# Two mixtures of experts: choice and counts made per sequence in the stage of the gate logits, normalised tiles and the inversion's products written by ScalarE, list of experts made over partitions

## What is computed

```
x = x + recurrent_block(norm(x))        # projections, gated linear recurrence, feed-forward
x = x + moe0(norm(x))                   # 16 experts of width 256, 2 per token, relu
x = x + attention(norm(x))              # 16 heads of 8, rotary
x = x + block(norm(x))                  # attention, x1 = norm(.)*g1+be1, moe1(x1), norm
# moe0: logits = y @ Wg + bg + bias; the two highest; weights = softmax of these two
# moe1: p = softmax(x1 @ Wg + bg) over 8 experts of width 512 (gelu); the two highest,
#       divided by their sum
# out[token] = sum over its two experts of weight * (act(y @ W1[e] + b1[e]) @ W2[e] + b2[e])
```

## Time and profile before

| | us |
|---|---|
| median of 3 runs (2523.53 to 2530.19) | 2529.16 |
| the profiled execution | 2531.16 |
| its span | 2529.3 |
| TensorE busy | 2030.4 (80%) |
| VectorE busy | 1988.9 (79%) |
| ScalarE busy | 1507.4 (60%) |
| GpSimd busy | 593.3 (23%) |

### The profile page before, as it was taken

How to read it: one execution, slowest core, us unless ns; L and a number is a source line. 1 busy time by engine, 2 the same in 40 slices (tenths; PEclk the granted TensorE clock), 3 DMA queues, 4 the chain that set the end, 5 groups by cost and what they waited for, 6 DMA issues and landing times. The chain is left out here.

```text
span 2529.3 us, 45491 instructions
## 1 busy us (share of the span) xinstructions
PE 2030.4 (80%) x16896; PEld 958.9 (38%) x16896; DVE 1988.9 (79%) x3319; ACT 1507.4 (60%) x2948; POOL 593.3 (23%) x702
## 2 busy tenths in 40 slices
PE   6999675882479999999999579999999999369910
PEld 4888464771222222222222322222222222359910
DVE  7887647565679999999994779999999994576635
ACT  5553330340118988989888218988989889105500
POOL 2444300667520000000000340000000000316555
PEclk9999885895769999999999769999999999559955
DMA  5000010243341010110100351010110100302211
GB/s 192 1 1 1 0 32 11 78 91 78 115 147 32 20 42 19 33 42 20 42 6 10 110 153 31 21 42 19 32 42 20 42 6 10 122 10 74 64 51 55
DMA packets 94411, 121.16 MB, mean 48 GB/s; under 512 B 23664, under 2 KB 56560, under 8 KB 93936
## 3 DMA queue, kind: packets, MB, share of 16 engines
q1 hardware_dynamic: 73712, 78.92, 11.3%
q0 software_dynamic: 8960, 18.37, 3.0%
q10 hardware_dynamic: 11520, 20.98, 2.7%
HBM read 69.70 MB, written 42.99 MB: 45 GB/s over the span
## 5 line engine op out<-in xcount | busy, mean ns | idle before, releaser
L1489 DVE TENSOR_REDUCE mx<-psum 128x1 f32<-128x1024 f32 x1024 | 1175.1, 1216 | 82.2 <-PE psum L1377 81.3
L1466 ACT ACTIVATE p<-psum 128x512 f32<-128x512 f32 x2048 | 1102.5, 596 | 108.8 <-PE psum L1399 66.2
L1411 PE MATMUL psum<-p,v_ext 128*32 128x256 f32 x8192 | 656.5, 392 | 39.3 <-ACT p L1466 39.2
L1377 PE MATMUL psum<-ks,qs 64*128 64x512 bf16 x2048 | 636.0, 395 | 53.1 <-DVE mx L1489 29.9
L1399 PE MATMUL psum<-qs,ks 64*128 64x512 bf16 x2048 | 630.6, 383 | 1.5 <-ACT p L1466 1.3
L1411 PEld LDWEIGHTS psum<-p,v_ext 128*32 128x32 f32 x8192 | 162.2, 108 | 474.2 <-ACT p L1466 254.6
L1279 POOL CAST m_near<-mx 128x16 bf16<-128x16 f32 x128 | 25.1, 196 | 1080.9 <-DVE mx L1489 1076.8
L1399 PEld LDWEIGHTS psum<-qs,ks 64*128 64x128 bf16 x2048 | 123.4, 93 | 404.0 <-ACT p L1466 368.0
L746 ACT ACTIVATE hid<-psum,stage 128x128 f32<-128x128 f32 x448 | 132.1, 366 | 180.3 <-PE psum L716 180.3
L690 POOL DMA_INDIRECT x_in<-n_rows,token_of x152 | 166.2, 1093 | 296.3 <-POOLq L85 229.2
L1377 PEld LDWEIGHTS psum<-ks,qs 64*128 64x128 bf16 x2048 | 118.7, 94 | 115.3 <-DVE mx L1489 81.3
(11 more groups left out here) (229 smaller groups left out, 2120.7 us busy)
## 6 DMA issues: line engine op xcount, KB each, us to landing
qs<-qk_parts SPq DMA_DIRECT2D x128, 104.0 KB
ks<-qk_parts SPq DMA_DIRECT2D x128, 104.0 KB
qk_parts<-piece__1 ACTq DMA_DIRECT2D x40, 256.0 KB, 3.7
qk_parts<-piece__2 ACTq DMA_DIRECT2D x40, 256.0 KB, 3.5
answers<-y_out SPq DMA_DIRECT2D x152, 64.0 KB, 1.5
ew<-in_moe SPq DMA_DIRECT2D x1, 5136.0 KB, 18.8
ew<-in_moe SPq DMA_DIRECT2D x1, 4624.0 KB, 13.9
n_rows<-n_all SPq DMA_DIRECT2D x8, 512.0 KB, 3.2
```

Source lines behind the costliest of these rows:

```text
L1377: pe.matmul(psum[:, bank, :], a["qs"][r, g % NKF, j % KM, i * P:(i + 1) * P], a["ks"][r, g % NKF, j % KM, k * HALF:(k + 1) * HALF], start= ...
L1411: last = pe.matmul(psum[GR * j:GR * j + VW, O_BANK, q], t["v_ext"][:, b * NT + i, VE * (h0 + j):VE * (h0 + j) + VW], a["p"][:, (GH * s + j ...
L1466: act.activation(a["p"][:, n % NP, :], psum[:, S_BANK + n % NS, :], ACT.Exp, scale=DH ** -0.5)\
L1489: dve.tensor_reduce(a["mx"][:, g % 2, h, j, 0, c:c + 1], psum[:, bank:bank + 2, :].rearrange("p a c -> p (a c)"), AX.X, ALU.max)\
```

## The change

- `gate_logits` becomes `choose`. The normalised tiles are written by ScalarE (`normalise`), with scale 1/std and a shift that VectorE computes by one more small operation in `scale`. ScalarE's order is root(b+1), normalise(b), both copies of b; in the second mixture the four exponentials stand behind all of it.
- The choice, the one-hot rows and their sum (`pick`) are made per sequence by VectorE in that stage: in the first mixture behind each sequence's logits, in the second for all four behind the last logits. TensorE counts per sequence (`count`), behind all its other work, into banks 6 and 7.
- `route` begins with the counts. The weights of the mix are made at its end. The list of experts is made with the tile's number along the partitions (128x16 or 128x8), and TensorE turns it at the beginning of `invert`, where VectorE reads it behind its last chunk.
- In `invert` VectorE writes 8 comparisons in one instruction (`hi_eq`, 128 x 8 x 80 or 72), and ScalarE multiplies each with the token's number.
- `ew` of both mixtures is loaded behind `consts` at the start of the mixture. `consts` has its own semaphore, which VectorE and TensorE wait for within `choose`; `ew` is waited for ahead of `route`.

```diff
 def route(nc, t, layer, E, tiles):
...
+    with stage(nc, "step", "to_exp", "exped") as (block, step, to_exp, exped):
+        if not layer:
+            @block.scalar
+            def _(act):
+                act.wait_ge(to_exp, 1)
+                act.activation(tmp[:, :, 1], tmp[:, :, 0], ACT.Exp).then_inc(exped, 1)
...
+            if not layer:
+                dve.tensor_tensor(tmp[:, :, 0], mx[:, :, 1], mx[:, :, 0], ALU.subtract).then_inc(to_exp, 1)
+            link(dve.tensor_copy(cnt[:, :, :], psum[:, 7, 0:TE].rearrange("p (t e) -> p e t", e=E)))
...
             dve.tensor_copy(t["slot_of"][:, :, :], sel[:, :, :])
+            link(dve.tensor_scalar(t["ended"][:, 0:E], end[:, 0:E], t["token"][:, 0:1], None, ALU.is_lt))
+            link(dve.tensor_reduce(t["who"][:, :], t["ended"][:, 0:E], AX.X, ALU.add))
+            if layer:
+                link(dve.tensor_tensor(tmp[:, :, 0], mx[:, :, 0], mx[:, :, 1], ALU.add))
+                link(dve.reciprocal(tmp[:, :, 1], tmp[:, :, 0]))
+                link(dve.tensor_tensor(wt[:, :, :], mx[:, :, 0:2], tmp[:, :, 1:2].to_broadcast([P, T, 2]), ALU.mult))
+            else:
+                dve.wait_ge(exped, 1)
+                link(dve.tensor_scalar(tmp[:, :, 0], tmp[:, :, 1], 1.0, None, ALU.add))
+                link(dve.reciprocal(wt[:, :, 0], tmp[:, :, 0]))
+                link(dve.tensor_tensor(wt[:, :, 1], tmp[:, :, 1], wt[:, :, 0], ALU.mult))
...
+    hi_eq = t["hi_eq"]
+    with stage(nc, "step", "lo_ready", "eq_ready", "hi_ready", "used", "named") as \
+            (block, step, lo_ready, eq_ready, hi_ready, used, named):
+        @block.scalar
+        def _(act):
+            for n in range(pairs):
+                if n % G == 0:
+                    act.wait_ge(eq_ready, n // G + 1)
+                if n >= 2 * G:
+                    act.wait_ge(used, n - 2 * G + 1)
+                act.activation(t["hi_hot"][:, n % (2 * G), 0:tiles], hi_eq[:, n // G % 2, n % G, :], ACT.Copy,
+                               scale=t["token"][:, n // 2:n // 2 + 1]).then_inc(hi_ready, 1)
...
-                for n in range(c * G, (c + 1) * G):
-                    dve.tensor_scalar(t["hi_hot"][:, n % (2 * G), 0:tiles], t["iota"][:, 0:tiles],
-                                      flat(hi)[:, n:n + 1], t["token"][:, n // 2:n // 2 + 1],
-                                      ALU.is_equal, ALU.mult).then_inc(hi_ready, 1)
+                if c >= 2:
+                    dve.wait_ge(hi_ready, G * (c - 1))
+                dve.tensor_tensor(hi_eq[:, c % 2, :, :], t["iota"][:, 0:tiles].unsqueeze(1).to_broadcast([P, G, tiles]),
+                                  flat(hi)[:, c * G:(c + 1) * G].unsqueeze(2).to_broadcast([P, G, tiles]),
+                                  ALU.is_equal).then_inc(eq_ready, 1)
+            dve.wait_ge(named, 1)
+            dve.tensor_scalar(t["expert_of"][:, 0:tiles], psum[0:1, 3, 0:tiles], float(t["E"] - 1), None, ALU.min)
             dve.wait_ge(used, pairs)
             link(dve.tensor_scalar(t["token_f"][:, 0:tiles], psum[:, 2, 0:tiles], -1.0, 0.0, ALU.add, ALU.max))
             dve.tensor_copy(t["token_of"][:, 0:tiles], t["token_f"][:, 0:tiles])
...
+            pe.transpose(psum[0:1, 3, 0:P], t["who"][:, :], t["ident"][:, :]).then_inc(named, 1)
             for n in range(pairs):
                 if n % G == 0:
                     pe.wait_ge(lo_ready, n // G + 1)
...
+def choose(nc, t, w, layer, E, x, n):
...
+            def normalise(b):
+                act.wait_ge(scales_ready, b + 1)
+                for i in range(NT):
+                    act.activation(n[b][:, i, :], src[b][:, i, :], ACT.Identity, scale=t["rstd"][:, b % 2, i:i + 1],
+                                   bias=t["shift"][:, b % 2, i:i + 1]).then_inc(tile_ready, 1)
+            def copy_turned(b):
                 for h in range(NH):
                     act.wait_ge(turned, NT * b + TPH * (h + 1))
                     if b:
                         act.wait_ge(done, NH * (b - 1) + h + 1)
                     act.activation(t["y_t"][:, h * HALF:(h + 1) * HALF], psum[:, 2 * (b % 2) + h, :], ACT.Copy)\
                         .then_inc(y_copied, 1)
+            def exponent(b):
+                act.wait_ge(to_exp, b + 1)
+                v = lg[:, b * NT:(b + 1) * NT, :]
+                act.activation(v, v, ACT.Exp).then_inc(exped, 1)
+            root(0)
+            for b in range(B):
+                if b + 1 < B:
+                    root(b + 1)
+                normalise(b)
+                copy_turned(b)
+                if layer and b == B - 1:
+                    for c in range(B):
+                        exponent(c)
...
+            def count(b):
+                pe.wait_ge(both_ready, b + 1)
+                c, v = slice(b * NT * E, (b + 1) * NT * E), both[:, b * NT:(b + 1) * NT, :].rearrange("p t e -> p (t e)")
+                pe.matmul(psum[:, 6, c], t["before"][:, :], v, start=True, stop=True)
+                pe.matmul(psum[:, 7, c], t["ones"][:, :], v, start=True, stop=True)
             for b in range(B + 1):
                 if b < B:
                     turn(b)
                 if b:
                     logits(b - 1)
+            pe.wait_ge(t["consts_loaded"], 16 * (layer + 1))
+            for b in range(B):
+                count(b)
...
+            def scale(b):
                 r, m, v = rstd[:, b % 2, :], tmp[:, 0, :], t["var"][:, b % 2, :]
                 dve.wait_ge(std_ready, b + 1)
+                if b >= 2:
+                    dve.wait_ge(tile_ready, NT * (b - 1))
                 link(dve.reciprocal(r, t["std"][:, b % 2, :]))
...
                 link(dve.tensor_tensor(r, r, m, ALU.mult))
-                for i in range(NT):
-                    dve.tensor_scalar(n[b][:, i, :], src[b][:, i, :], mv[:, b % 2, i, 0:1], r[:, i:i + 1],
-                                      ALU.subtract, ALU.mult).then_inc(tile_ready, 1)
+                dve.scalar_tensor_tensor(t["shift"][:, b % 2, :], mv[:, b % 2, :, 0], -1.0, r, ALU.mult, ALU.mult)\
+                    .then_inc(scales_ready, 1)
+            def take(b):
+                dve.wait_ge(done, NH * (b + 1))
+                i = slice(b * NT, (b + 1) * NT)
+                v = lg[:, i, :]
+                dve.tensor_tensor(v, psum[:, 4 + b % 2, 0:NT * E].rearrange("p (t e) -> p t e", e=E),
+                                  t["grow"](f"moe{layer}_bg", E), ALU.add).then_inc(added, 1)
+                dve.wait_ge(added, b + 1)
+                if layer:
+                    link(dve.tensor_reduce(tmp2[:, i, 0], v, AX.X, ALU.max))
+                    dve.tensor_tensor(v, v, tmp2[:, i, 0:1].to_broadcast([P, NT, E]), ALU.subtract).then_inc(to_exp, 1)
+                else:
+                    link(dve.tensor_tensor(v, v, t["grow"]("moe0_bias", E), ALU.add))
+            def pick(b):
+                s = slice(b * NT, (b + 1) * NT)
+                v, L3 = lg[:, s, :], [P, NT, E]
+                if layer:
+                    dve.wait_ge(exped, b + 1)
+                    link(dve.tensor_reduce(tmp2[:, s, 0], v, AX.X, ALU.add))
+                    link(dve.reciprocal(tmp2[:, s, 1], tmp2[:, s, 0]))
+                    link(dve.tensor_tensor(v, v, tmp2[:, s, 1:2].to_broadcast(L3), ALU.mult))
+                for i in range(b * NT, (b + 1) * NT):
+                    last = dve.max(mx[:, i, :], lg[:, i, :])
+                link(last)
+                for i in range(b * NT, (b + 1) * NT):
+                    last = dve.max_index(ix[:, i, :], mx[:, i, :], lg[:, i, :])
+                link(last)
+                link(dve.tensor_copy(sel[:, s, :], ix[:, s, 0:2]))
+                experts = t["iota"][:, 0:E].unsqueeze(1).to_broadcast(L3)
+                dve.tensor_tensor(oh0[:, s, :], experts, sel[:, s, 0:1].to_broadcast(L3), ALU.is_equal)
+                link(dve.tensor_tensor(oh1[:, s, :], experts, sel[:, s, 1:2].to_broadcast(L3), ALU.is_equal))
+                dve.tensor_tensor(both[:, s, :], oh0[:, s, :], oh1[:, s, :], ALU.add).then_inc(both_ready, 1)
+            measure(0)
+            for b in range(B):
+                if b + 1 < B:
+                    measure(b + 1)
+                scale(b)
                 if b >= 2:
-                    add_bias(b - 2)
-            for b in range(B - 2, B):
-                add_bias(b)
+                    take(b - 2)
+                    if not layer:
+                        if b == 2:
+                            dve.wait_ge(t["consts_loaded"], 16)
+                        pick(b - 2)
+            if layer:
+                dve.wait_ge(t["consts_loaded"], 32)
+                take(B - 2)
+                take(B - 1)
+                for b in range(B):
+                    pick(b)
+            else:
+                for b in range(B - 2, B):
+                    take(b)
+                    pick(b)
...
                 nc.sync.dma_start(to, of).then_inc(t["weights_loaded" if n < 4 else "first_loaded"], 16)
-            load_experts(0)
```

(46 more changed lines are left out.)

58 lines of the change are left out of this document (1 added, 57 removed).

## The result

The kernel after takes **2539.26 us** (median of 6 runs, 2537.76 to 2543.47) against 2529.18 us for the kernel before on the same chip: ratio **1.0048 [1.0037, 1.0058]**, slower by 10.1 us where +12.2 was forecast. The profiled spans are 2529.3 and 2536.9 us.

What follows compares the result with a forecast made beforehand. Each stage, closed by a barrier, costs its own longest chain; TensorE bounds the inversion. First mixture -6.1, second +19.3 and start -1 gave +12.2 us, a median of 2541.4 us, range 2529 to 2550.

Steps and rivals of the forecast that it cites:

- Step 1: Gate logits: tiles in ScalarE's order chain the sequences; last logits +4.9 us in the first mixture, +17.1 in the second.
- Step 2: Choice, one-hots and counts per sequence: first use of counts -5.0 us in the first mixture, +18.9 in the second.
- Step 3: List of experts over partitions, mix weights last: -2.0 us in the first mixture, -0.45 in the second.
- Step 4: Inversion, token products on ScalarE: TensorE stays the bound and starts later, +0.9 us in each mixture.
- Rival C: Inversion: ScalarE becomes the bound at 0.48 us a product, +3.5 us in each mixture, 2548.5 us; chance 0.08.
- B: Inversion: TensorE runs at full clock, -5 us in each mixture, 2531.5 us, no change; chance 0.08.
- Step 5: Program start: first mixture's experts loaded in the mixture instead, -1 us.
- Rival A: Gate stages: ScalarE's order does not chain sequences and they keep their pace, about -10 us, 2519 us; chance 0.10.

Runs made afterwards that it cites:

- tiles_ahead: Kernel after with only ScalarE's order changed: the tiles of the next sequence go ahead of the copies of the current one; ratio 0.9981 to the kernel before.
- covered_choice: tiles_ahead's order, VectorE measuring and scaling all sequences before taking and picking, second mixture choosing on the logits; ratio 0.9934 to the kernel before.
- experts_at_start: Kernel after with the load of the first mixture's experts back at the program's start; ratio 1.0047 to the kernel before.
- tiles_on_vector: Kernel after with the normalised tiles of both mixtures written by VectorE again; ratio 0.9973 to the kernel before.
- early_roots: covered_choice plus bf16_products, with ScalarE's roots of sequences 2 and 3 one place earlier; 2512.32 us against 2553.42 for the kernel before, ratio 0.9839.
- bf16_products: Kernel after with the inversion's one-hots and products in bfloat16, the token split into two exact parts; ratio 0.9972 to the kernel before.

## Why the prediction was right

The mechanism and the place were right: tiles_ahead shows that the later logits come from ScalarE's order, and covered_choice that the rest is the second mixture's uncovered picks. Step by step, forecast and measured:

```
                                   first mixture      second mixture
1 pace of a sequence              7.7      7.6        14.1     13.9
  last logits                    +4.9     +4.9       +17.1    +16.8
2 first use of the counts        -5.0     -5.5       +18.9    +17.8
3 list, weights, barrier         -2.0     -1.8        -0.45    -0.17
4 first product                  +0.9     +0.9        +0.9     +0.8
  sum                            -6.1     -6.4       +19.3    +18.5
5 start of the program           -1.0     -0.2
```

- *Step 1* held in every part: the tiles' 3.2 us, the copy released by TensorE, the root, and in the second mixture GpSimd's 4.77 us in the sum. tiles_ahead shows it by a change of order alone. (Two of the working's times in between are 0.15 us late, 2181.3 and 2195.4; its 2209.3 and the end follow without them.)
- *Step 2, a pick in the second mixture*: I took 3.6 us between 2.75 and 3.6; it is 3.39. Four of them make 0.8, most of the 1.1 us between +18.9 and +17.8. In the first mixture the last logits to the counts took 6.0 us against a forecast of 6.5 (400.5 less 394.0).
- *Step 3* was right for what it priced: list and weights went from 3.32 to 1.37 us in the first mixture (-2.0 forecast) and from 1.85 to 1.42 in the second (-0.45). What it left out is the barrier behind them: VectorE's idle time there went from 1.08 to 1.27 and from 0.64 to 0.91 us, which eats more than half of the second mixture's gain. Why the barrier takes longer stayed open.
- *Step 4* was right: TensorE stayed the bound. ScalarE's product takes 0.26 us (2.13 for eight), under TensorE's 0.43 and under the 0.3 that I took. Rival C (0.48 a product) fell by that line, and B by the clock of 0.50 in the stretch above. B's price used 0.35 us a product, for which no row stood and which is not the 0.3 of the forecast; by the 0.26 measured its gain would have been larger.
- *Step 5* was the one real miss: no gain shows, where 1 us was forecast. The -0.2 is inside the scatter of this stretch (355.5 to 358.1 us over the experiments' kernels), and the first product does not move (experts_at_start). SyncE's wait was for the small loads, and the earlier trace rows gave no sign that the large one behind them slowed it; I should have kept nothing as the value.
- *Rival A* (the gate stages keep their pace) is what tiles_on_vector made true: 0.9973, about 7 us faster, where A's working gave 10.

The error of 2.1 us of the median is smaller than the 4.4 us by which untouched stretches differed between the two profiled executions: the sum of the touched stages, +12.0 for +12.2, is the better test of the working than the median. That it fits to 0.2 us is in part luck: the mixtures came out 0.3 and 0.8 us under their forecasts, and the start 0.8 over its own.

## What to carry to other kernels

When work moves to another engine, write down that engine's whole queue: behind which waiting instruction does the moved work stand, and who needs it before that wait can end? The same instructions in another order were worth 15 us here, and moving work off an engine that already waits for another (VectorE in the inversion) was worth nothing. Splitting a step per sequence pays only where each part but the last lies under a wait; behind the last wait, four parts cost more than one whole (16.4 against 15.3 us from the last logits to the counts).

## What the hardware showed that I had not expected

- *VectorE stands still beside GpSimd.* Under a 128x1024 tensor_tensor of GpSimd, several kinds of VectorE's small operations last until that one ends. VectorE and GpSimd in the kernel after, second mixture:

```profile
2163.61 0.17 DVE L908 TENSOR_TENSOR rstd<-rstd,tmp 128x8 f32<-128x8 f32 x1
...
2163.73 2.34 POOL L808 TENSOR_TENSOR n_all<-n_all,rows 128x1024 f32<-128x1024 f32 x1 [13.07 <-ACT n_all L821]
...
2163.81 2.28 DVE L909 SCALAR_TENSOR_TENSOR shift<-mv_all,rstd 128x8 f32<-128x8 f32 x1
2166.01 1.25 DVE L892 BATCH_NORM_STATS2 stats<-n_all 128x6 f32<-128x128 f32 x6
```

 GpSimd's operation began at 2163.73 and ended at 2166.07 (VectorE's at 2166.09). The same instruction without it takes 0.17 us. Hit were tensor_tensor, scalar_tensor_tensor, tensor_scalar and a cast (1.03 us at 2207.72 in covered_choice, to 2208.75; GpSimd's ended at 2208.72). Not every kind is: BATCH_NORM_STATS2 ran at its usual 0.2 us each, and in covered_choice a reciprocal at 2195.50 took its 0.20 us, and a tensor_tensor with one input in PSUM, at 2205.56, its 0.23, both under GpSimd's. The kernel before had three such stalls in the second mixture, 5.9 us in all. They were not hidden: each ended with GpSimd's pair, and the 2.89 us that GpSimd then waited are the rest of the scaling and the tiles. So this stall, and not GpSimd's 4.8 us alone, made the pace of 7.65 us; it is read off the trace, and no run took it out of the kernel before. In the kernel after one such stall is left, the one shown, beside a longer chain of ScalarE's; they counted again once the order of ScalarE was repaired. Moving the roots so that the stalls fall elsewhere gave 3.2 us (early_roots), and there the first pairs follow at 5.66 us.
 The Trainium skill (VectorE: DVE Perf Modes, Two Vector instructions with no wait between them) says that VectorE's second read interface is shared with GpSimd, and that an instruction reads through it if two of its inputs are in SBUF, or if it has one and runs in a mode with two ports. The trace agrees with the first part: two inputs in SBUF are hit, one of two in PSUM is not. That the tensor_scalar and the cast, with one input each, ran in such a mode no run here shows.
- *The clock stayed at its lower level through 27.57 us of products without a gap*: granted clock 0.50 (1.2 GHz) in every kernel with float32 products. At the last counts of the first mixture the granted clock differed between kernels with the same instructions there (0.50 in the kernel after, a mean of 0.83 to 0.90 over the 3 to 5 us around them in experts_at_start, bf16_products and tiles_ahead); the counts come 6.0 us after the last logits at the lower clock and 5.5 at the higher one. What decides between them stayed open.
